# Session-weighted projection, fp8 feed-forward: one-product spread of the maximum, first products in three banks, another order of the first units

## The reference

```
xm  = x * (channel < channel_counts[b])          # channel_counts is the input _lenS
h   = gelu(W_sess[id[b]].T @ xm + b_sess[id[b]])   # 256 x 2048
o   = (W2.T @ h + b2) * (time < seq_lens[b])       # 128 x 2048
w_scale = 448 / max|weight|;  w_q = fp8e4m3(weight * w_scale)     # 2048 x 2048
x_scale = 57344 / max|o| over all batches;  q = fp8e5m2(o * x_scale)
out = x + (q @ w_q.T) / x_scale / w_scale + bias                  # 128 x 2048 per batch
```

## Time and profile before

| what | value |
|---|---|
| median of 3 runs | 848.15 us |
| the profiled execution | 847.79 us, its span 846.0 us |
| TensorE busy | 832.6 us (98%) |
| VectorE, ScalarE, GpSimd busy | 479.9, 320.1, 444.2 us |
| HBM traffic | 252 GB/s over the span |
| last unit of stage one, project1 starts | 390.50 us |
| first product of stage two starts | 398.74 us |

### The profile page before, as it was taken

The page is one execution under the profiler, slowest core; times in us unless marked ns, Lnnn a source line. Parts: engine busy times, 40 slices in busy tenths (PEclk is TensorE's granted clock), DMA queues, the critical chain, the costliest instruction groups (busy, mean ns, idle before and its releaser), DMA issues.

```text
span 846.0 us, 9980 instructions
## 1 busy us (share of the span) xinstructions
PE 832.6 (98%) x3467; PEld 471.2 (56%) x3502; DVE 479.9 (57%) x495; ACT 320.1 (38%) x334; POOL 444.2 (53%) x195
## 2 busy tenths in 40 slices
PE   7999999999999999999999999999999999999998
PEld 4767676767767676675444444444444444444443
DVE  6889998888888888888532323232323232332322
ACT  5767777889888898884000000000000000000000
POOL 3634343799999999996632333323242424242321
PEclk9999999999999999999999999999999999999999
DMA  7799997676768866655569686867677676768672
GB/s 272 289 374 421 354 350 277 241 291 256 299 256 340 337 254 246 260 221 212 201 203 282 215 280 215 279 211 273 225 258 242 242 258 225 277 213 285 217 248 100
DMA packets 73022, 222.06 MB, mean 262 GB/s; under 512 B 37402, under 2 KB 39202, under 8 KB 52642
## 3 DMA queue, kind: packets, MB, share of 16 engines
q1 hardware_dynamic: 72994, 221.71, 73.1%
HBM read 144.35 MB, written 69.21 MB: 252 GB/s over the span
## 4 chain that ended last, share of the span: by engine, by line
PE 91%; DMA 3%; DVE 3%; issue 1%; POOL 1%; SPq 1%; ACT 1%; DVEq 0%
PE ps_h L804 50%; PE ps_h L720 19%; PE ps_o L736 12%; PE ps_o L731 10%; DMA split_w<-wqT 1%; DMA lens_i<-in_itok_B 1%; DVE hl L557 0%; DMA wraw<-split_w 0%; DMA x_sb<-x_sb 0%; DVE whl L523 0%; DVE x_sb L647 0%; DVE o_sb L567 0%; SPq L263 0%; POOL xl L406 0%; DVE wc L583 0%
## 5 line engine op out<-in xcount | busy, mean ns | idle before, releaser
L804 PE MATMUL ps_h<-wqT,x_sb 128*128 128x512 bf16 x2014 | 440.8, 379 | 2.7 <-DMA x_sb<-x_sb 0.8
L804 PEld LDWEIGHTS ps_h<-wqT,x_sb 128*128 128x128 fp8e5 x2048 | 200.1, 98 | 242.9 <-issue 2.2
L406 POOL TENSOR_TENSOR xl<-x_sb,xh 128x1024 fp32r<-128x1024 f32 x62 | 149.5, 2411 | 85.5 <-ACT xh L448 85.5
L720 PE MATMUL ps_h<-xh,whl 128*128 128x512 f32 x508 | 159.8, 436 | 3.6 <-DVE hl L557 2.4
L430 POOL TENSOR_TENSOR h<-h,bias_sb 128x2048 f32<-128x2048 f32 x16 | 73.3, 4579 | 139.0 <-DMA h<-in_x 139.0
L430 POOL TENSOR_TENSOR x_sb<-x_sb,bias_sb 128x2048 f32<-128x2048 f32 x16 | 72.3, 4519 | 139.9 <-DMA x_sb<-in_x 139.9
L670 DVE SCALAR_TENSOR_TENSOR o_sb<-ps_h,scales,h 128x512 f32<-128x512 f32 x64 | 48.0, 751 | 155.2 <-PE ps_h L804 155.2
L670 DVE SCALAR_TENSOR_TENSOR o_sb<-ps_h,scales,x_sb 128x512 f32<-128x512 f32 x64 | 47.8, 750 | 145.1 <-PE ps_h L804 145.1
L720 PEld LDWEIGHTS ps_h<-xh,whl 128*128 128x128 f32 x508 | 96.1, 190 | 51.6 <-issue 31.1
L736 PE MATMUL ps_o<-h,w_sb 128*128 128x512 f32 x256 | 120.3, 592 | 0.0
L567 DVE SCALAR_TENSOR_TENSOR o_sb<-ps_o,b_sb,steps 128x1024 f32<-128x1024 f32 (+1 forms) x65 | 82.2, 1265 | 32.0 <-PE ps_o L736 31.8
(11 more groups left out here) (79 smaller groups left out, 452.9 us busy)
## 6 DMA issues: line engine op xcount, KB each, us to landing
x_sb<-in_x SPq DMA_DIRECT2D x47, 1024.0 KB, 5.2
masked_out<-o_sb SPq DMA_DIRECT2D x32, 1024.0 KB, 5.4
o_in<-masked_out SPq DMA_DIRECT2D x32, 1024.0 KB, 8.9
out<-o_sb SPq DMA_DIRECT2D x31, 1024.0 KB, 5.1
h<-in_x SPq DMA_DIRECT2D x16, 1024.0 KB, 7.1
wt<-in_L_ffn_weight SPq DMA_DIRECT2D x42, 384.0 KB, 5.4
wqT<-in_L_ffn_weight SPq DMA_DIRECT2D x19, 832.0 KB, 8.1
wraw<-split_w SPq DMA_DIRECT2D x28, 256.0 KB, 5.0
```

The costliest lines, as they stand in the source:

```text
L406: pool.tensor_tensor(xl[:, u % 2, :], x_cols(u), xh[:, u % 2, :].bitcast(fp32), ALU.subtract)\
L720: mm = nc.tensor.matmul(to[:, cols], whl[:, b % DIRECT, rows], xs[:, u % 2, cols], start=(k == 0), stop=(k == 2))
L804: mm = nc.tensor.matmul(ps_y[n], qT[:, r, k // 2, :, k % 2], wq[:, n, k, :], start=(k == 0), stop=(k == KT - 1))
```

## The change

SP's first loads are reordered; ScalarE takes over the high half of session weight 0 and the rounded copy of unit 1; VectorE's first instructions are reordered; project0 waits for hl only before its third product, and hidden(2, 0) for hl of unit 0 only; the mask of batch 4's weights moves from the end of ScalarE's round 5 into round 6, behind gelu0(7).

```diff
+    CUT_TILES = (2, 2, 4, 4, 4)          # tiles in each cut of batch 0; 5 cuts in place of 4
+    FIRST_PAIR = ((0, 0), (0, 1), (0, 2), (1, 0), (0, 3), (1, 1), (1, 2), (1, 3))
+    FIRST_DONE = [1 + max(s for s, (b, n) in enumerate(FIRST_PAIR) if b == r) for r in range(2)]
+    TAIL = [slice(BANK * (NC - 1), BANK * NC - BANK // 2), slice(BANK * NC - BANK // 2, BANK * NC)]
-    WARM_SCALE, WARM_STEP, WARM_QUANT = 8, 2, 4
+    WARM_SCALE, WARM_STEP = 8, 4
+        ps_tail = [ps_h[:, 1, BANK:BANK + BANK // 2], ps_o[:, 1, BANK:BANK + BANK // 2]]
-        o_row, o_all = ps_h[0:1, 1, 0:P], ps_h[:, 1, P:P + 1]
+        o_row = ps_h[:, 1, 0:P]
...
@@ SP: start
+            load_x_part(0)
             sp.dma_start(counts_i[:, :], counts.partition_broadcast(P)).then_inc(counts_loaded, 16)
-            load_x_part(0)
...
             load_session_weight(0)
+            sp.dma_start(b2_sb[:, :], b2.rearrange("(p a) -> p a", a=1)).then_inc(b2_loaded, 16)
             load_x_part(1)
             sp.dma_start(w2_sb[:, :, :], w2.rearrange("(j p) s -> p j s", p=P)).then_inc(params_loaded, 16)
+            sp.dma_start(lens_i[:, :], lens.partition_broadcast(P)).then_inc(lens_loaded, 16)
             load_session_weight(1)
             load_x(1)
-            (lens_i and b2_sb were loaded here)
...
@@ SP: ahead of the loop of stage two (turn = DMA transpose, store_y = store of a batch)
+            sp.wait_ge(q_ready, CUTS)
+            load_o(2, 0)
+            sp.wait_ge(q_ready, 1 + CUTS)
+            turn(1)
+            load_o(3, 1)
+            sp.wait_ge(y_psum, FIRST_DONE[0] + ONE)
+            sp.wait_ge(q_ready, 2 + CUTS)
+            turn(0)
+            for r in range(2):
+                sp.wait_ge(y_ready, FIRST_DONE[r] + FREE4)
+                store_y(r, r)
+                load_x_again(2 + r, r)
-            with sp.Fori(0, STEPS - 1) as i:
+            with sp.Fori(1, STEPS - 1) as i:
...
@@ ScalarE
+            act.wait_ge(raw_loaded[0], 16)
+            act.wait_ge(const_step, 2)
+            act.activation(whl[:, 0, 0:HID], raw_sb[0], ACT.Copy, scale=cmask[:, 0:1]).then_inc(wh_direct, 1)
+            act.wait_ge(x_first[1], 16)
+            act.activation(xh[:, 1, :], x_cols(1), ACT.Copy).then_inc(xh_ready, 1)
             act.wait_ge(hbias_ready, 1)
             gelu0(0)
...
+                if u == UPB * (DIRECT - 1):
+                    mask_session_weight(DIRECT)
...
-                if u % UPB == 1 and DIRECT <= (u + 3) // 2 < B:
+                if u % UPB == 1 and DIRECT < (u + 3) // 2 < B:
                     mask_session_weight((u + 3) // 2)
...
@@ VectorE: start (ident and ident_f now here; xl of unit 0; low half of weight 0; W2; xl of unit 1)
-            split_session_weight(0)
+            (ident, ident_f)
             dve.wait_ge(xh_ready, 1)
             (xl of unit 0)
-            (xh of unit 1, xl of unit 1)
+            low_session_weight(0)
             (w2h, w2l)
-            (lens_f, start_i)
+            (xl of unit 1)
+            split_session_weight(1)
             split_h_rest(0)
-            for b in range(1, DIRECT):
+            for b in range(2, DIRECT):
                 split_session_weight(b)
+            (lens_f, start_i)
...
@@ VectorE: between the stages
-            dve.tensor_reduce(o_one[:, :], o_row, AX.X, ALU.max).then_inc(o_one_ready, 1)
-            dve.wait_ge(o_amax_psum, 1)
-            dve.reciprocal(o_rec, o_all).then_inc(scale_step, 1)
+            dve.tensor_reduce(o_amax, o_row, AX.X, ALU.max).then_inc(scale_step, 1)
+            dve.reciprocal(o_rec, o_amax).then_inc(scale_step, 1)
...
-            for i in range(UNITS - 2 - QUANT, CHUNKS):
+            late = range(UNITS - 2 - QUANT, CHUNKS)
+            round_at(late[0])
+            quantize(1, 1, True, slice(0, T))
             (o_inv, y_scale)
+            for i in late[1:]:
                 round_at(i)
+            for y, (b, n) in enumerate(FIRST_PAIR):
+                if y == FIRST_DONE[0]:
+                    quantize(0, 2, True, slice(0, T))
+                dve.wait_ge(xb_ready, b + 1)
+                evacuate(b, slice(n * BANK, (n + 1) * BANK), ps_y[y % NC], y)
...
@@ TensorE
-                    if u > 1:
+                    if u == 2:
+                        pe.wait_ge(hl_ready, 1)
+                    if u > 2:
                         pe.wait_ge(hl_ready, u)
...
-                pe.wait_ge(hl_ready, u + 1)
+                if u == 1:
+                    pe.wait_ge(hl_ready, u + 1)
+                pe.wait_ge(h0_gelu, u + 1)
...
+                    if k == 2:
+                        pe.wait_ge(hl_ready, u + 1)
...
-            nc.tensor.matmul(o_row, o_pmax, ident_f[:, :], start=True, stop=True).then_inc(o_row_psum, 1)
+            nc.tensor.matmul(o_row, o_pmax.broadcast_to((P, P)), ident_f[:, :], start=True, stop=True)\
+              .then_inc(o_row_psum, 1)
             stay_warm(WARM_STEP)
-            pe.wait_ge(o_one_ready, 1)
-            nc.tensor.matmul(o_all, ones[:, :], o_one[:, :], start=True, stop=True).then_inc(o_amax_psum, 1)
-            stay_warm(WARM_QUANT)
...
+            together = [n for b, n in FIRST_PAIR[0:NC - 1]]
+            turn_cut(0)
+            for k in range(CUTS):
+                if k + 1 < CUTS:
+                    turn_cut(k + 1)
+                pe.wait_ge(q_widened, k + 1)
+                for n in together:
+                    mm = products(ps_y[n], 0, n, CUT_KS[k])
+            for y, (b, n) in enumerate(FIRST_PAIR):
+                if y < len(together):
+                    continue
+                if y == len(together):
+                    pe.wait_ge(qT_loaded[1], 16 + DMA)
+                pe.wait_ge(w_rounded, QUARTER[n])
+                pe.wait_ge(y_ready, y + 1)
+                products(ps_y[y % NC], b, n, range(KT)).then_inc(y_psum, 1)
...
+                        if last and r == 1 and n == NC - 1:
+                            for bank, cols in zip(ps_tail, TAIL):
+                                products(bank, r, n, range(KT), slice(cols.start - n * BANK, cols.stop - n * BANK))\
+                                    .then_inc(y_psum, 1)
```

More of the change, by code:

```diff
@@ L388, in _ @@
                 sp.wait_ge(y_stored[r], 16 * (STEPS - r) + DMA)
-            for n in range(NC):
+            for n in range(NC + 1):
                 sp.wait_ge(y_chunk_stored[n], 16)
@@ L666, in step2 @@
                     dve.wait_ge(y_stored[r], i * 16 + DMA)
-                    for n in range(NC):
-                        cols = slice(n * BANK, (n + 1) * BANK)
-                        dve.wait_ge(y_psum, b * NC + n + 1 + ONE)
-                        dve.scalar_tensor_tensor(y_sb[:, r, cols], ps_y[n], y_scale, x2[r][:, cols],
-                                                 ALU.mult, ALU.add).then_inc(y_ready, 1)
-            for r in range(2):
-                dve.wait_ge(o_stored[r], 16 * STEPS)
-            with dve.Fori(0, STEPS - 1) as i:
+                    for n in range(NC - 1):
+                        evacuate(r, slice(n * BANK, (n + 1) * BANK), ps_y[n], b * NC + n)
+                    if last and r == 1:
+                        for h, cols in enumerate(TAIL):
+                            evacuate(r, cols, ps_tail[h], B * NC - 1 + h)
+                    else:
+                        evacuate(r, slice((NC - 1) * BANK, F), ps_y[NC - 1], b * NC + NC - 1)
+            with dve.Fori(1, STEPS - 1) as i:
                 step2(i, False)
@@ L787, in _, with products @@
                                           start=True, stop=True)
                 mm.then_inc(q_turned, 1)
+            def products(bank, r, n, ks, cols=slice(0, BANK)):
+                for k in ks:
+                    mm = nc.tensor.matmul(bank, qT[:, r, k // 2, :, k % 2], wq[:, n, k, cols],
+                                          start=(k == 0), stop=(k == KT - 1))
+                return mm
+            together = [n for b, n in FIRST_PAIR[0:NC - 1]]
[5 more added lines that the diff above has]
+                for n in together:
+                    if k == 0:
+                        pe.wait_ge(w_rounded, QUARTER[n])
+                    mm = products(ps_y[n], 0, n, CUT_KS[k])
+                    if k == CUTS - 1:
+                        mm.then_inc(y_psum, 1)
```

114 lines of the change are left out of this document (61 added, 53 removed).

## The result

The changed kernel takes 841.81 us (median of 842.12, 842.65, 841.39 and 841.49), the kernel before 848.17 on the same chip: ratio 0.9917, 95% interval 0.9896 to 0.9938. One execution of all, of the kernel with the banks in the old order, ran slow (1151.49 us, at a granted clock of 0.70) and is left out.

A forecast was written before the change was run, and what follows sets the result against it. TensorE, busy 98% of the span, was taken to bound the kernel. The terms 1.37 + 1.25 + 0.34 + 0.05 + 1.22 + 0.40 = 4.63 us off the profiled 847.79 gave a median of 843.5, range 842.6 to 845.9.

The forecast's parts named there:

- Start and mask: Stage one: 1.37 us won at the start (units 0 to 1) and 1.25 at batch 4's mask (units 6 to 7).
- The cost of 0.2 for a later first product: Start of stage one: counts load later, so the first product comes at 8.4 us, before 8.22 (bounds 0 and 0.7).
- what is late next is nothing within 1 us: Mask of batch 4: once it moves, nothing else there is late within 1 us, so 1.25 us is won.
- the prediction's own sign of being wrong: Wrong if TensorE waits at bank four or five, first units exceed 5.9 us apart, or the loop waits for transposes.
- The spread maximum: Between the stages: one product spreads the maximum, the second product and its waits go; 0.34 us won (0.2 to 0.5).
- First products in three banks: Start of stage two: first cut of 256 columns, 12 tiles turned between products; 0.05 us won (-0.5 to 0.3).
- Bank 3 later: Stage two: batch 1's first bank before batch 0's last, batch 1 quantized early; 1.22 us won (-1 to 1.22).
- The last bank: End of the kernel: last bank halved, so last evacuation and store are shorter; 0.40 us won (0.2 to 0.7).
- (c): Last bank: half-width products don't hide their weight loads, 16 more loads, 1.57 us more, 845.1 us; chance 0.05.
- (a): Start of stage two: batch 1's transpose or the last weight chunk comes late, 844.4 to 846.5 us; chance 0.17.
- (b): Stage one: the start gives nothing, as ScalarE or hl of unit 2 paces the first units, 844.9 us; chance 0.12.
- (d): Stage two's loop: SP runs later, each batch's transpose lands late, slower than before, 852.5 us; chance 0.03.

## Why the prediction was right and where it was wrong

**The step that failed.** The prediction said that "a change that removes no product can win only gaps and what stands ahead of the first and behind the last product", and so it had no term for the pace of the units in which nothing waits. The runs showed that this pace went from 5.887 to 5.873 us: 0.13 us up to unit 10 and 0.74 in the 53 units from there to unit 63, 0.87 together. (Another 0.11 of the second line of the table is one short wait near unit 52 that is gone.) With these 0.87 taken back the median would be 842.7, just inside the range. The cause is the tile o_one that the diff removes ahead of all large ones, which puts W2 and its columns 32 bytes apart modulo 64; I read that line as a saved instruction only. The range had bounds for the terms that I had, and nothing stood for a term that I had not.

**Start and mask.** Their sum came out near: 2.62 predicted, 2.81 in the pair of profiles with the 0.13 just named; over the traces, project1 of unit 10 comes at 80.2 (median of the seven kernels with the mask in its old place) and 77.6 (of the twelve with start and mask as in the changed one), 2.6 us apart. That is luck, as two errors cancel: in the pair the start gave 2.12 (project1 of unit 1 at 25.67 and 23.55) and not 1.37, and the mask 0.56 (1.25 lost before, 0.69 after) and not 1.25.

In the start, the 1.57 us between units 0 and 1 went as said. The cost of 0.2 for a later first product did not come: project1 of unit 0 is 0.54 us earlier in this pair. That the first product itself did not come later is an accident of the trace before, in which session weight 0 is split only at 7.82, behind its load. In five of the seven traces with the old start this load is earlier and the first product comes between 6.9 and 7.1 us; in all thirteen with the new start it comes between 7.6 and 8.5. So the usual first product is about 1 us later, more than the 0.2. It costs nothing, because in those five traces TensorE then waits 0.2 to 2.5 us for hl of unit 0 ahead of project0(0). None of the eleven traces with the new lists and project0's new wait has this wait; the two with the new lists alone have 0.8 and 1.3 us of it. Three rows: that load in the trace before, then in the one with the mask alone, and the wait for hl in the latter.

```profile
7.82 0.35 DVE L523 TENSOR_SCALAR whl<-o_in,cmask 128x256 fp32r<-128x256 f32 x1 [1.98 <-DMA o_in<-in_L_cond_W_sess]
```

```profile
6.49 0.35 DVE L525 TENSOR_SCALAR whl<-o_in,cmask 128x256 fp32r<-128x256 f32 x1 [0.61 <-DMA o_in<-in_L_cond_W_sess]
14.70 0.47 PE L733 MATMUL ps_o<-hh,w2l 128*128 128x512 f32 x1 [1.08 <-DVE hl L559]
```

Project1 of unit 1 measures the whole of the start: 25.67 and 23.32 as medians of the seven traces and of the thirteen, 2.4 us apart. (The first products follow each other every 0.43 us and later ones every 0.23, with a granted clock of 1.00 in either stretch of the traces before and after; the moment at which this changes lies anywhere from 7 to 14 us in the traces, and moves the first units too.)

I also took the 0.73 us of the earlier trace rows for the conversion's own time. It ended at 5.22 whether counts came at 4.49 or, in the run with project0's new wait alone, at 4.84: 0.04 us behind the end of a GpSimd memset (the memset in the kernel before, then the conversion in that run; timeline). Landing at 5.30, behind the memset, it took 0.18.

```profile
3.39 1.79 POOL L402 MEMSET steps<- 128x2048 bf16 x1
```

```profile
4.84 0.38 DVE L530 CAST counts_f<-counts_i 128x32 f32<-128x32 int32 x1 [4.84 <-DMA counts_i<-in__lenS]
```

For the mask, the step "what is late next is nothing within 1 us" failed: 0.45 to 2.7 us stay lost in units 6 to 9 of the kernels with the moved mask, and the prediction's own sign of being wrong, first units over 5.9 us apart, is there with 5.98, 6.14 and 6.19. I had looked at the semaphores of the chain, not at the DMA share of 0.97 to 0.98 around it (38 to 100 us of the kernel before).

**The spread maximum.** 0.42 at the first cut in both kernels against 0.34, though in the kernel before only 0.12 of it reached the first product; of two fp32 weight loads at 0.19, less than one is in the open.

**First products in three banks.** The sum was 0.05 and the term came out at -0.36, inside its bounds: 0.31 gained ahead of the first product, 0.67 us between the first product and batch 2 for the turns (0.8 predicted). The 0.53 that are missing ahead of the first product are GpSimd's addition, which holds the ports until 393.35 while the first cut has started at 392.62. The rule that the prediction weighed for the second quantize ("SBUF — State Buffer", section "Who interferes with whom", of the Trainium skill) struck here, where I had not applied it. For the second quantize it cost TensorE nothing: VectorE came first at 396.31, took 1.28 us, and GpSimd's add beside it 2.61 us instead of 1.65.

**Bank 3 later.** Right: 1.22 gained, no wait at banks four and five. The chunks were done at 406.80, 14.2 us behind the first cut; my 410 to 411.5, on the clock of the trace before, are 13.6 to 15.1 behind it. The order alone is worth 1.5 us, so the banks' order and not the early quantizing hides the chunks.

**The last bank.** 0.78 against 0.40, above the bound of 0.7: 0.27 for the evacuation as said, and 0.55 behind it, most of that the landing, 1.9 to 2.0 us for 128 KB where 256 KB took 2.5. I had taken 0.13 from bounds of 0 to 0.5. Rival (c) is refuted: the half products start every 0.11 us, and their weight loads hide.

**Rivals (a), (b) and (d)** did not come: the transposes landed at a median of 9.0 us, in time; the start gave more, not less; the loop's batches are 13.81 us apart as before.

## What to carry to other kernels

Before pricing a diff, list what it does to the addresses of tiles and not only to instructions; a removed tile of 32 bytes was worth 0.9 us here, and one unused tile tests for it in either direction. A short VectorE instruction that looks long in a trace may have stood behind one of GpSimd: look at what GpSimd runs beside it before taking its length as a price. Where the DMA share is near 1.0, taking one late transfer out of the chain can make the next one late, and what is lost there differs between executions by more than the edit gives: read such a gap, and the landing of the first loads, in several traces before pricing them.

## What the runs showed of the hardware

- The distance of fp32 products depends on where weights and columns lie modulo 64 bytes: the same 22 products take 5.873 us with W2 32 bytes apart from its columns and 5.887 with all alike, and 5.913 in the one trace with W2 alike and whl apart. A second pace of 5.893 us comes and goes with the tiles unmoved, for a reason that is open.
- A short VectorE instruction pays for what is left of a long GpSimd one: a conversion of 128 x 32 elements 0.73 and 0.38 us beside a memset and 0.18 alone, a cut of 256 columns 0.88 beside an addition and 0.35 alone (one of 512 columns 0.78 and 0.48), the product of two single columns (y_scale) 1.41 beside an addition that ended 0.02 us ahead of it.
- Not every instruction pays: the reciprocal of a single column just ahead of y_scale took 0.16 us beside the same addition.
- A store of 128 KB landed after 1.9 to 2.0 us, one of 256 KB after 2.4 to 2.5.
